# One root instead of two in the second layer norm of a small language-model tower

## The reference

```python
h = h + attn(layernorm(h), Q, E)          # 8 heads, linear attention: mask * (s Q s^T), times (E s)
h = h + ffn(layernorm(h), ...)            # causal softmax attention, then 8 experts of which 2 count

def layernorm(x, eps=1e-05):              # over the last axis, 64 values
    return (x - mean(x)) / sqrt(var(x) + eps)

def ffn(x, ...):
    h = rmsnorm(x, ln1_w)                 # v * rsqrt(mean(v * v) + 1e-6) * w
    q, k, v = rope(h @ wq.T), rope(h @ wk.T), h @ wv.T
    x = x + softmax(causal(q k^T / 4)) v @ wo.T
    flat = rmsnorm(x, ln2_w)
    return x + sum over experts of gate[e] * (silu(flat @ w1[e].T) * (flat @ w3[e].T)) @ w2[e].T
```

## Time and profile before

| | |
|---|---|
| median of 3 runs | 262.43 us |
| the profiled execution | 261.8 us |
| its span, first to last instruction | 260.1 us |
| PE busy | 225.7 us, 87% |
| DVE busy | 181.6 us, 70% |
| ACT busy | 163.3 us, 63% |
| POOL busy | 148.2 us, 57% |
| granted TensorE clock | 1.000 throughout |
| chain that ended last | PE 50%, DVE 27%, ACT 9%, issue 9%, POOL 3% |

### The profile page before, as it was taken

How to read it: one execution, slowest core, us unless ns; L and a number is a source line. 1 busy time by engine, 2 the same in 40 slices (tenths; PEclk the granted TensorE clock), 3 DMA queues, 4 the chain that set the end, 5 groups by cost and what they waited for, 6 DMA issues and landing times.

```text
span 260.1 us, 6594 instructions
## 1 busy us (share of the span) xinstructions
PE 225.7 (87%) x2456; PEld 156.2 (60%) x2465; DVE 181.6 (70%) x428; ACT 163.3 (63%) x293; POOL 148.2 (57%) x189
## 2 busy tenths in 40 slices
PE   8978879879998999997688788997689898999986
PEld 3645446447685786885566566763346465566665
DVE  4137557942478578678998977956988669986582
ACT  2478763769877597763455436565667966666660
POOL 6997001113377575374083678568887576677780
PEclk9999999999999999999999999999999999999999
DMA  2576100000000000000000000000000000000010
GB/s 42 142 179 145 39 4 1 3 0 0 3 1 3 0 0 4 3 1 0 3 0 3 0 3 1 3 3 0 0 5 4 0 3 20 3 13 10 3 25 20
DMA packets 7467, 4.48 MB, mean 17 GB/s; under 512 B 6500, under 2 KB 6796, under 8 KB 7436
## 3 DMA queue, kind: packets, MB, share of 16 engines
q1 hardware_dynamic: 7436, 4.06, 6.7%
HBM read 3.53 MB, written 0.52 MB: 16 GB/s over the span
## 4 chain that ended last, share of the span: by engine, by line
PE 50%; DVE 27%; ACT 9%; issue 9%; POOL 3%; DVEq 0%; ACTq 0%; POOLq 0%
PE bank L1242 48%; DVE nmx L1032 3%; DVE shared L1205 3%; ACT shared L719 1%; ACT qT L607 1%; DVE early L779 1%; DVE shared L890 1%; ACT early L498 1%; PE bank L1460 1%; POOL shared L406 1%; DVE s L882 1%; DVE oT L1059 1%; ACT shared L587 1%; DVE ex L1040 1%; ACT qT L732 1%
## 5 line engine op out<-in xcount | busy, mean ns | idle before, releaser
L1242 PE MATMUL bank<-early 64*64 64x256 f32 (+4 forms) x561 | 58.2, 352 | 11.6 <-DVE early L779 2.7
L406 POOL TENSOR_TENSOR shared<-shared 128x512 f16<-128x512 f32 x44 | 51.0, 1159 | 18.4 <-ACT shared L719 17.0
L1242 PEld LDWEIGHTS bank<-early 64*64 64x64 f32 (+3 forms) x561 | 31.3, 126 | 30.3 <-issue 5.4
L1205 DVE SCALAR_TENSOR_TENSOR shared<-bank,qT 128x512 f32<-128x512 f32 x44 | 30.1, 688 | 13.7 <-ACT qT L732 12.3
L344 POOL TENSOR_TENSOR stat<-stat,neghalf 128x4 f32<-128x4 f32 x16 | 16.2, 1012 | 37.6 <-DVE stat L864 28.2
L732 ACT ACTIVATE qT<-bank 128x512 f32<-128x512 f32 x44 | 26.2, 597 | 13.7 <-PE bank L1242 13.6
L1242 PE MATMUL bank<-qT,shared 128*128 128x256 f32 x112 | 31.2, 388 | 3.9 <-DVE shared L890 3.1
L719 ACT CAST shared<-shared 128x512 f16<-128x512 f32 x44 | 27.0, 614 | 7.8 <-DVE shared L1205 7.3
L1242 PE MATMUL bank<-onehot,w3h 128*128 128x512 f16 x88 | 26.3, 380 | 3.7 <-DVE shared L1205 3.4
L439 POOL TENSOR_TENSOR oTx<-oT,oTx 128x512 f16<-128x512 f32 x16 | 19.0, 1188 | 18.0 <-ACT oTx L619 18.0
L1242 PE MATMUL bank<-onehot,w1h 128*128 128x512 f16 x88 | 26.2, 379 | 0.0
(11 more groups left out here) (225 smaller groups left out, 490.2 us busy)
## 6 DMA issues: line engine op xcount, KB each, us to landing
early<-in_tcn_w_dram SPq DMA_DIRECT2D x2, 320.0 KB, 4.4
w1s<-in_w1m_dram SPq DMA_DIRECT2D x2, 256.0 KB, 3.7
qT<-in_w3m_dram SPq DMA_DIRECT2D x2, 256.0 KB, 3.5
out_dram<-L SPq DMA_DIRECT2D x8, 64.0 KB, 1.9
qw<-in_attn_q_dram SPq DMA_DIRECT2D x2, 128.0 KB, 2.9
hTs<-in_w2m_dram SPq DMA_DIRECT2D x1, 256.0 KB
cos<-in_cos_t_dram SPq DMA_DIRECT2D x2, 96.0 KB, 2.3
sin<-in_sin_t_dram SPq DMA_DIRECT2D x2, 96.0 KB, 2.6
```

Of the source, the lines that this page charges most:

```text
L406: nc.gpsimd.tensor_tensor(hhx[:, i, 1, :], hh[:, u % RING, :], hhx[:, i, 0, :], ALU.subtract).then_inc(S["lo_ready"], 1)
L1205: V_.scalar_tensor_tensor(hh[:, u % RING, :], bank[2 + u % 2][:, :], HH_SCALE / FFN_SCALE, sil[:, u % 2, :], ALU.mult, ALU.mult).then_inc( ...
L1242: return nc.tensor.matmul(out_, l_, r_, start=a, stop=z, skip_group_check=skip)
```

## The change

The change makes both roots of the second layer norm in one POOL operation. Since `a*a = 1/(S/64 + 1e-5)`, the argument of the second root is `S/(S/64 + 1e-5)/64 + 1e-6`, which DVE works out in `ln2_b` with a reciprocal, a product and a scale and add; POOL then takes the power of both rows of `stat` at once (128x2x4), and `ln2_c` makes `xf` and right behind it `hr`. `ln2_d` is gone. For pair 3 the split of `hr` goes from DVE to POOL (`second_split(3)` at b = 2, after `head_sum(0)`), `rows(3)` and `qkv(3)` use bank 1, the bank of the stacks, stacks 8 to 11 stand two places earlier, `max_rows(4)` no longer waits for the rotary step of pair 3, and that step stands on DVE after `max_out(4)` and no longer before `share(4)`.

```diff
-        QKV_BANK = (5, 5, 2, 0)
-        STACK_B = {(1, 0): 6, (1, 1): 7, (2, 1): 8, (2, 2): 9, (3, 0): 10, (3, 1): 11, (4, 1): 12, (4, 2): 13,
+        QKV_BANK = (5, 5, 2, 1)
+        STACK_B = {(1, 0): 6, (1, 1): 7, (1, 2): 8, (2, 0): 9, (2, 1): 10, (2, 2): 11, (4, 1): 12, (4, 2): 13,
                    (5, 0): 14, (5, 1): 15}
...
-            def variance2_root(p):
-                inverse_root(12, 11, p, "var2_ready", "rstd2_ready")
-
-            def square2_root(p):
-                inverse_root(6, 5, p, "q1_ready", "rinv_ready")
+            def both_roots(p):
+
+                g4 = slice(4 * p, 4 * p + 4)
+                pool.wait_ge(S["var2_ready"], p + 1)
+                nc.gpsimd.tensor_tensor(stat[:, 13:15, g4], stat[:, 11:13, g4],
+                                        neghalf[:, 0:4].unsqueeze(1).to_broadcast([P, 2, 4]), ALU.pow) \
+                    .then_inc(S["rstd2_ready"], 1)
...
                 if s == 1 and p:
                     first_h(p)
                     if p:
-                        variance2_root(p - 1)
+                        both_roots(p - 1)
                 if s == 2 and p:
-                    square2_root(p - 1)
-                if s == 3:
-                    if p:
-                        second_split(p - 1)
-                    if p + 2 < PAIRS:
-                        variance_root(p + 2)
+                    second_split(p - 1)
+                if s == 3 and p + 2 < PAIRS:
+                    variance_root(p + 2)
...
                 if b == 1:
-                    variance2_root(3)
-                    square2_root(3)
+                    both_roots(3)
+                if b == 2:
+                    second_split(3)
...
             def ln2_b(p):
                 if p:
                     dve.wait_ge(S["hr_ready"], p)
-                centre(p, h[:, 4 * p:4 * p + 4, :], cenB[:, :, :], sqrB[:, :, :], 11, "var2_ready")
+                g4 = slice(4 * p, 4 * p + 4)
+                centre(p, h[:, 4 * p:4 * p + 4, :], cenB[:, :, :], sqrB[:, :, :], 11, "q1_ready")
+                dve.wait_ge(S["q1_ready"], p + 1)
+                link(V_.reciprocal(stat[:, 10, g4], stat[:, 11, g4]))
+                link(V_.tensor_tensor(stat[:, 10, g4], stat[:, 10, g4], stat[:, 9, g4], ALU.mult))
+                V_.tensor_scalar(stat[:, 12, g4], stat[:, 10, g4], 1.0 / V, 1e-6, ALU.mult, ALU.add) \
+                    .then_inc(S["var2_ready"], 1)
 
             def ln2_c(p):
...
-                link(V_.tensor_tensor(xf[:, g4, :], cenB[:, :, :], bc4(stat[:, 12, g4]), ALU.mult))
-                link(V_.tensor_tensor(stat[:, 10, g4], stat[:, 12, g4], stat[:, 12, g4], ALU.mult))
-                link(V_.tensor_tensor(stat[:, 10, g4], stat[:, 10, g4], stat[:, 9, g4], ALU.mult))
-                V_.tensor_scalar(stat[:, 5, g4], stat[:, 10, g4], 1.0 / V, 1e-6, ALU.mult, ALU.add) \
-                    .then_inc(S["q1_ready"], 1)
-
-            def ln2_d(p):
-                g4 = slice(4 * p, 4 * p + 4)
-                dve.wait_ge(S["rinv_ready"], p + 1)
+                link(V_.tensor_tensor(xf[:, g4, :], cenB[:, :, :], bc4(stat[:, 13, g4]), ALU.mult))
                 if p:
                     dve.wait_ge(S["hsplit_ready"], p)
-                V_.tensor_tensor(hrB[:, :, :], xf[:, g4, :], bc4(stat[:, 6, g4]), ALU.mult) \
+                V_.tensor_tensor(hrB[:, :, :], xf[:, g4, :], bc4(stat[:, 14, g4]), ALU.mult) \
                     .then_inc(S["hr_ready"], 1)
...
-                if b == 3:
-                    rotary(3)
...
+                if b == 3:
+                    rotary(3)
...
-                if b == 2:
-                    ln2_d(3)
-
-                    dve.wait_ge(S["hr_ready"], PAIRS)
-                    dve.wait_ge(S["trh_ps"], PAIRS - 1)
-                    link(V_.tensor_copy(shlB[:, :, 0, :], hrB[:, :, :]))
-                    V_.tensor_tensor(shlB[:, :, 1, :], hrB[:, :, :], shlB[:, :, 0, :], ALU.subtract) \
-                        .then_inc(S["hsplit3_ready"], 1)
...
-                before = (("logits_read", 2), ("v_ready", 1), ("q_ready", TILES), ("nmT_ready", 4))[p]
+                before = (("logits_read", 2), ("v_ready", 1), ("q_ready", TILES), ("stk_ready", 12))[p]
...
-                if b == 4:
-                    pe.wait_ge(S["v_ready"], PAIRS)
```

More of the change, by code:

```diff
@@ L1016, in _ @@
                         mask_omega(g + 1)
-                        ln2_d(p - 1)
                         rotary(p - 2)
                 if s == 3:
-                    if p == 1:
-                        ln2_d(0)
                     if p + 2 < PAIRS:
@@ L1424, in rows @@
             def rows(p):
-                if p < 3:
-                    pe.wait_ge(S["hsplit_ready"], p + 1)
-                else:
-                    pe.wait_ge(S["hsplit3_ready"], 1)
-                before = (("logits_read", 2), ("v_ready", 1), ("q_ready", TILES), ("nmT_ready", 4))[p]
+                pe.wait_ge(S["hsplit_ready"], p + 1)
+                before = (("logits_read", 2), ("v_ready", 1), ("q_ready", TILES), ("stk_ready", 12))[p]
                 pe.wait_ge(S[before[0]], before[1])
```

## The result

The changed kernel takes 266.28 us (median of 4, 265.94 to 268.15) beside 262.47 for the kernel before (262.27 to 262.62): ratio 1.016 [1.013, 1.019]. The direction was forecast; the time lies 1.6 us above the 264.7 of the forecast and 0.7 above the range.

What follows compares the result with a forecast made beforehand. Bound by PE waiting on DVE masks in the first attention, then row maxima and POOL's pair-3 parts before stack(12). Terms 0.60 + 0.40 + 0.60 + 0.70 = 2.3, tail 0: 262.43 + 2.3 = 264.7 us, range 262.5 to 265.6.

Steps and rivals of the forecast that it cites:

- g = 6, 10, 14: First attention, masks of pairs 0 to 2: three added ln2_b instructions ahead of each, costing 0.60, 0.40 and 0.60 us.
- g = 15: First attention, mask behind the 128x2x4 root: root 1.75 us instead of 1.01, less 0.04 saved, step +0.70 us.
- Rival 3: The root is all fixed cost (1.01), the rest as forecast: 264.0 us; inside the forecast's own chance of 0.63.
- Gain 0: Second attention: rotary(3) starts at 148.4 against 148.15, so savings do not reach the chain; gain 0, between -0.3 and +0.5 us.
- The wait before stack(12): Second attention, PE: 2.4 us gained at max_rows(4) become a wait before stack(12), which stays at 156.5.
- stack(8) "hidden": Second attention, (1, 2): PE waits 0.45 us for stack(8), hidden by the 0.60 of ln2_b(3); without that cover 0.45.
- The port beside VectorE's casts: Second attention: POOL's head_sum(0) beside row_max(3)'s four small casts on DVE; at most 0.6 us, taken as 0.
- Rival 4: stack(8) 0.45 and port 0.6 both strike on top of 2.3, root 2.02 another 0.3: 266.0 us; chance 0.12.
- the signs that I named beforehand: Wrong if mask g = 15 to rotary(3) (33.2 us) shrinks over 1, mask shifts don't add, or the stack(12) wait is short.

Runs made afterwards that it cites:

- after_again: The changed kernel run once more, nothing altered: 266.60 us, ratio 1.015 to the kernel before.
- head_back: The changed kernel with two roots in the old order for pairs 0 to 2, one root kept for pair 3: 262.90 us, ratio 1.002 to the kernel before.
- fill: The changed kernel with 11 useless 128x512 matmuls on PE ahead of stack(12): 265.18 us, ratio 1.009 to the kernel before.
- fill3: The changed kernel with three useless 128x512 matmuls in TensorE's wait before stack(12): 265.12 us, ratio 1.010 to the kernel before.
- rotary_early: The changed kernel with rotary(3) back ahead of share(4) and max_out(4) on DVE: 263.38 us, ratio 1.003 to the kernel before.
- two_early: The changed kernel with two roots for pairs 0 to 2 and rotary(3) ahead of share(4): 261.16 us, ratio 0.994 to the kernel before.
- head_late: head_back with useless small VectorE operations: three ahead of masks g=6, 10, 14, two ahead of g=11, 15: 266.59 us, ratio 1.015 to the kernel before.
- stacks_only: The kernel before with only the new places for stacks 8 to 11: 263.61 us, ratio 1.003 to the kernel before.
- roots_behind: mask_first with POOL's root behind the remainder of oT (L441) and the split one tile later: 261.71 us, ratio 0.996 to the kernel before.
- mask_first: rotary_early with small operations behind masks g=6, 10, 14 and masks g=11, 15 ahead of xf: 263.27 us, ratio 1.002 to the kernel before.
- late_zero: The kernel of head_back once more, as zero of a delay series: 263.39 us, ratio 1.006 to the kernel before; 5 of 12 runs slowed.

## Why the prediction missed, step by step

- **g = 6, 10, 14: right.** Forecast 0.60, 0.40, 0.60; measured 0.60 at mask 6, 0.42 at the query behind mask 10 (2.43 late there in all, less 1.41 and 0.60), and 0.61 at mask 14 (1.63 less 1.02).
- **g = 15: right in kind, too large.** The root was put at 1.75, it takes 1.64; the step was put at 0.70 and is 0.50 at the mask, and 0.2 of slack on TensorE, which I had taken for none, leaves 0.3. Head 1.9 in place of 2.3. Rival 3 (all fixed cost) is refuted by the root's own row, 1.64 us for 128x8 against 1.01 for 128x4.
- **"Gain 0" of the second attention: wrong by 0.4.** The places were right: counted from the first row maximum, as the prediction counts, max_rows(4) runs at 147.95 in after_again (forecast 148.0) and rotary(3) at 148.47 (forecast 148.4). Before, it was 148.15. I called that equal; most of the loss was in my working, and I rounded it away. With 0.1 more in C, B + C is 0.40 longer in after_again and 0.42 in head_back, both at full clock up to stack(12).
- **The wait before stack(12): the step that failed.** "The 2.4 us that PE gained at max_rows(4) turn into a wait in front of stack(12)" was right, and it was counted as idle time that costs nothing: "`stack(12)` stays at 156.5". What follows a wait was taken to run as fast as before. Up to that wait the time was as forecast: counted from mask g = 4, stack(12) comes at 158.8 in after_again, the very figure of the forecast (with the head 0.4 under it and the second attention 0.4 over). Behind it D is 4.15 where 2.52 was taken for granted, because the clock falls to the 1.2 GHz level. fill and fill3 show that filling the wait gives 1.1 to 1.5 back, rotary_early and two_early that removing it does, and head_late that the loss of the clock doesn't need the single root.
- **stack(8) "hidden": nearly.** In the changed kernel 0.15 comes through at row_max(3) (after_again); without the cover of `ln2_b(3)` it is 0.42 (stacks_only), for which the prediction had 0.45. Row_max(4) comes 24.6 after the first row maximum (after_again), where I put 24.2 (143.4 - 119.17).
- **The port beside VectorE's casts: it shows, with 0.38.** The four small operations of row_max(3) last 0.81 us before and 1.19 in after_again. Its two casts take 0.42 and 0.32 where 0.18 was usual, and each ends just after the operation of POOL's head_sum(0) beside it:

```profile
142.15 0.42 DVE L1035 CAST ex<-nmx 128x8 bf16<-128x8 f32 x1
142.81 0.32 DVE L1037 CAST ex<-nmr 128x8 bf16<-128x8 f32 x1
142.08 0.46 POOL L391 TENSOR_TENSOR oT<-oT 128x128 f32<-128x128 f32 x1
142.62 0.47 POOL L392 TENSOR_TENSOR idx<-oT,xf 128x128 f32<-128x128 f32 x1
```

  The sum had 0 for it and the range up to 0.6. At row_max(4) it is the other way round: the first cast took 0.48 before and takes 0.18 now. Max_rows(4) still comes at the forecast time, so it is not shown that any of it reaches further.

The sum without the clock: 1.9 + 0.4 = 2.3, which is the forecast's 2.3 by two errors that cancel, and is what fill3 shows (265.12 - 262.80). With D's 1.6 it is 3.9; measured 3.8. Rival 4 had 266.0, near the measured 266.3, but by other terms: it had the root at 2.02, stack(8) at 0.45 and the port at 0.6 on top, and no fall of the clock. Its number is luck. Of the signs that I named beforehand, none fired: the shifts add up, the wait was long, and mask g = 15 to rotary(3) is 34.3 (33.2 before; 1.0 of the difference is the second clock drop). A check on what runs behind the wait was missing.

## What to carry to other kernels

A wait on TensorE that is "off the bill" is still a risk: price what comes behind it at both clocks. Put an operation that waits for its input behind what TensorE waits for, in each queue that it stands in: roots_behind gained 1.2 us in the head on mask_first (49.41 to 48.20) by moving the root behind another instruction on POOL, with the split after it. When a change bundles a head and a tail, time the halves: here the head's half, with the single root for pairs 0 to 2, lost 1.9 us, and the other half with one step moved (two_early) was a gain of 0.6%.

## What the hardware showed that I had not expected

- POOL's power of -0.5 takes 1.01 us for 128x4 and 1.64 for 128x8, and two of 128x4 start 0.98 apart: splitting costs 0.37.
- TensorE's granted clock went to the 1.2 GHz level behind a wait of 1.74 us preceded by another of 0.73 with only two transposes between (after_again), and 1.6 us were lost in D; in the profiles of head_back and late_zero, with the same two waits (0.74 and 1.75, 0.73 and 1.75), it stayed at 2.4 GHz.
- Three matmuls of no use, 0.7 us, in such a wait went with a mean clock of 0.999 or 1.000 in four of six runs (fill3), where all nine runs of the changed kernel without them had 0.994 or less.
- A cast of 128x8 on VectorE takes 0.18 us, and 0.42, 0.32 or 0.48 beside an operation of POOL (after_again, before).
